# Row maxima of an attention stage transferred in two halves of key heads

## What is computed

```python
x = x + _L0_attn_ref(_layernorm(x), ...)            # mixer
x = x + _L0_xattn_ref(_layernorm(x), ctx_512, ctx_512)
x = x + _L0_ffn_ref(_layernorm(x), ...)             # experts

def _L0_xattn_ref(q, k, v):      # 32 query heads, 8 key heads, 16 wide
    scores = jnp.einsum('bkgsd,bktd->bkgst', qh, kh) * scale
    attn = jax.nn.softmax(scores, axis=-1)
    out = jnp.einsum('bkgst,bktd->bkgsd', attn, vh)
```

## Time and profile before

| | us |
|---|---|
| median of 3 runs | 1469.41 (1467.95 to 1471.85) |
| the profiled execution, whole | 1465.78 |
| its span | 1464.0 |
| attention in it | 699 to 990 |

### The profile page before, as it was taken

One profiled execution on the slowest core, in us unless ns is written; L12 is line 12 of the kernel. 1 busy time (PEld: TensorE's weight loads), 2 busy tenths in 40 slices (PEclk: granted clock), 3 DMA queues, 4 the chain that ended last, 5 costly groups with the idle time before them and its releaser, 6 DMA issues.

```text
span 1464.0 us, 23008 instructions
## 1 busy us (share of the span) xinstructions
PE 1339.8 (92%) x7713; PEld 734.7 (50%) x7713; DVE 877.2 (60%) x1822; ACT 723.4 (49%) x1390; POOL 584.7 (40%) x871
## 2 busy tenths in 40 slices
PE   5799999999999999998788877888999999999997
PEld 4566666666666665654333333323444444444443
DVE  5798898979797979757888888755111111111111
ACT  2666667667666776663676766672111111111110
POOL 1454465555455465774223246143122222222221
PEclk9899999999999999998798988887999999999999
DMA  9000000000000000000210100002343344244322
GB/s 337 9 8 5 7 6 1 12 1 12 1 9 4 8 6 8 17 1 1 97 34 33 35 33 31 30 31 74 115 132 107 79 133 135 51 130 130 58 44 30
DMA packets 40291, 73.00 MB, mean 50 GB/s; under 512 B 18544, under 2 KB 22896, under 8 KB 39152
## 3 DMA queue, kind: packets, MB, share of 16 engines
q1 hardware_dynamic: 30240, 48.10, 9.4%
q0 software_dynamic: 8736, 20.61, 7.3%
q10 hardware_dynamic: 1200, 2.82, 0.5%
HBM read 148.91 MB, written 19.99 MB: 115 GB/s over the span
## 4 chain that ended last, share of the span: by engine, by line
PE 67%; DVE 18%; issue 5%; POOL 3%; ACT 3%; DMA 2%; SPq 1%; POOLq 0%; DVEq 0%; ACTq 0%
PE work_ps L535 13%; PE gate_ps L1524 9%; PE up_ps L1524 9%; PE down_ps L1508 9%; PE work_ps L607 7%; DVE conv L816 6%; PE work_ps L540 3%; PE work_ps L629 3%; DVE maxes L1216 3%; PE work_ps L1042 2%; PE mturn_ps L540 2%; PE decay_ps L1033 2%; PE decay_ps L617 2%; DVE mix L732 2%; DMA qT<-nmaxT 1%
## 5 line engine op out<-in xcount | busy, mean ns | idle before, releaser
L535 PE MATMUL work_ps<-xnT,w_in 128*128 128x256 f32 (+1 forms) x1216 | 301.0, 393 | 2.3 <-DVE xdt L856 1.5
L732 POOL TENSOR_TENSOR mix<-decay,cbm 128x512 f32<-128x512 f32 x128 | 182.1, 1424 | 218.9 <-ACT decay L727 191.0
L535 PEld LDWEIGHTS work_ps<-xnT,w_in 128*128 128x128 f32 (+1 forms) x1216 | 220.2, 189 | 64.9 <-issue 33.7
L723 ACT ACTIVATE decay<-decay_ps 128x512 f32<-128x512 f32 x256 | 154.1, 602 | 111.1 <-PE decay_ps L617 110.5
L1612 POOL DMA_INDIRECT out_dram<-y_out,ids x39 | 61.9, 1587 | 334.3 <-DVE row_w L1576 230.2
L1216 DVE TENSOR_REDUCE maxes<-work_ps 128x2 f32<-128x512 f32 x256 | 166.7, 683 | 42.8 <-PE work_ps L1018 41.8
L816 DVE SCALAR_TENSOR_TENSOR conv<-raw,conv_w,conv 128x256 f32<-128x256 f32 x240 | 179.2, 753 | 7.1 <-ACT conv L683 1.3
L1114 ACT ACTIVATE prob<-decay_ps 128x512 f32<-128x512 f32 x256 | 142.9, 608 | 78.9 <-PE decay_ps L1033 77.5
L1591 DVE TENSOR_TENSOR act<-gelu,up_ps 128x512 f32<-128x512 f32 x39 | 26.8, 688 | 252.1 <-PE up_ps L1524 252.1
L727 ACT ACTIVATE decay<-decay 128x512 f32<-128x512 f32 x256 | 164.0, 641 | 4.7 <-PE work_ps L535 3.0
L1524 PE MATMUL gate_ps<-w_e,xgT 128*128 x312 | 140.5, 593 | 1.4 <-ACT xgT L1541 1.0
(11 more groups left out here) (270 smaller groups left out, 1913.5 us busy)
## 6 DMA issues: line engine op xcount, KB each, us to landing
w_e<-c_experts_dram SPq DMA_DIRECT2D x39, 3072.0 KB
normed_tokens<-r_xn SPq DMA_DIRECT2D x17, 256.0 KB, 2.2
out_dram<-x_sb SPq DMA_DIRECT2D x17, 256.0 KB, 2.5
x_sb<-x_dram SPq DMA_DIRECT2D x1, 3072.0 KB, 16.6
w_in<-c_w_inT_dram ACTq DMA_DIRECT2D x1, 2560.0 KB, 12.3
w_in<-c_w_inT_dram SPq DMA_DIRECT2D x1, 2048.0 KB, 8.8
w_out<-c_w_outT_dram SPq DMA_DIRECT2D x1, 2048.0 KB, 21.6
RT<-cum_scratch SPq DMA_DIRECT2D x32, 48.0 KB
```

The costliest lines, as they stand in the source:

```text
L535: m = e.matmul(ps[0:width, at:at + L], w_in[:, k, col:col + width], xnT[b % 2][:, k, :], start=(k == 0), stop=(k == KD - 1))
L723: e.activation(decay[s % 5][:, :], decay_ps[s % 3][:, :], ACT.Relu, scale=-1.0).then_inc(piece_done[stage], 1)
L732: return e.tensor_tensor(four(mix[s % 5]), four(decay[s % 5]), cb, ALU.mult)
```

## The change

The order of the sweeps becomes key head first, tile second. The maxima of a batch are handed over in two halves h of key heads (0 to 3 and 4 to 7). nmax, n_turn, n_copy and n_out exist once per half: nmax in slots 12 and 28, n_turn in 13 and 29, n_copy and n_out in 14 and 30. Each half has buffers of its own (nmaxT), two transfers of 8 rows each, and a count of its own; the first score of each half of a batch waits for its half.

```diff
--- before.py
+++ after.py
@@ -42,6 +42,7 @@
 ITEMS = [(kh, par, t, quad) for kh in range(2) for par in range(2) for t in range(TPB) for quad in range(4)]
 ODD = [(quad + par) % 2 for kh, par, t, quad in ITEMS]
 LEAD = 5
+HALF = QH // 2
 NORMED = [(0, 2, -44, 0), (2, 4, -43, 1), (4, 8, 4, 2), (8, 16, 37, 5)]
 ROUTED = [(3, 0, 8), (5, 8, 12), (6, 12, 14), (7, 14, 16)]
 ROUND = 1.5 * 2.0 ** 23 * P
@@ -49,7 +50,8 @@
 def sweeps():
-    left = [[(t, k) for t in range(TPB) for k in range(KVH)] for odd in range(2)]
+
+    left = [[(t, k) for k in range(KVH) for t in range(TPB)] for odd in range(2)]
     order = []
     for p in range(len(ITEMS)):
         odd = 1 - ODD[(p - LEAD) % len(ITEMS)]
@@ -246,8 +248,10 @@
             put(r + 17 + 5 * t, ("q_copy_v", b, t, 0), ("q_turn", b, t, 1))
             put(r + 19 + 5 * t, ("q_copy_s", b, t, 1))
             put(n * (b - 1) + 6 + t, ("v_in", b, t))
-        put(n * (b - 1) + n - LEAD + 1, ("nmax", b), ("n_turn", b))
-        put(n * (b - 1) + n - LEAD + 2, ("n_copy", b), ("n_out", b))
+        for h in range(2):
+            put(n * (b - 1) + n // 2 * (h + 1) - LEAD + 1, ("nmax", b, h))
+            put(n * (b - 1) + n // 2 * (h + 1) - LEAD + 2, ("n_turn", b, h))
+            put(n * (b - 1) + n // 2 * (h + 1) - LEAD + 3, ("n_copy", b, h), ("n_out", b, h))
         if b == 1:
             put(2, ("first_expert",))
         for g in range(4):
@@ -456,7 +460,7 @@
             v_aug = [sb(st, f"v_aug{i}", [P, TPB, KVH, 32]) for i in range(2)]
             maxes = [sb(st, f"maxes{i}", [P, TPB, QH]) for i in range(2)]
             nmax = [sb(st, f"nmax{i}", [P, TPB, QH], F16) for i in range(2)]
-            nmaxT = [sb(st, f"nmaxT{i}", [QH, L], F16) for i in range(2)]
+            nmaxT = [[sb(st, f"nmaxT{i}_{h}", [HALF, L], F16) for h in range(2)] for i in range(2)]
             ctx.append(sb(st, "ctx2", [P, TPB, KVH, DH]))
             qT = [sb(st, f"qT{i}", [P, NPR, L], F16) for i in range(2)]
             kT = [sb(st, f"kT{i}", [P, KVH, L], F16) for i in range(2)]
@@ -1018,17 +1022,17 @@
                     m = e.matmul(work(*piece)[:, hh * L:(hh + 1) * L], qT[b % 3][base:base + PARTS, 2 * k + hh, t * P:(t + 1) * P], kT[b % 3][base:base + PARTS, k, :], start=True, stop=True)
                 m.then_inc(piece_done[stage], 1)
             elif stage == "n_turn":
-                b, = key
-                e.wait_ge(*done("nmax", b))
+                b, h = key
+                e.wait_ge(*done("nmax", b, h))
                 for t in range(TPB):
-                    m = e.transpose(work16(*piece)[0:QH, t * P:(t + 1) * P], nmax[b % 2][:, t, :], ident16[:, :])
+                    m = e.transpose(work16(*piece)[0:HALF, t * P:(t + 1) * P], nmax[b % 2][:, t, h * HALF:(h + 1) * HALF], ident16[:, :])
                 m.then_inc(piece_done[stage], 1)
             elif stage == "score":
                 s, = key
                 b, (kh, par, t, quad) = s // N_ITEMS, ITEMS[s % N_ITEMS]
                 base, k = SLOT * ODD[s % N_ITEMS], 4 * kh + quad
-                if s % N_ITEMS == 0:
-                    e.wait_ge(load_max, 32 * (b + 1))
+                if s % (N_ITEMS // 2) == 0:
+                    e.wait_ge(load_max, 32 * (2 * b + kh + 1))
                 e.wait_ge(*(done("exponent", s - 3) if s >= 3 else done("bound", NS_STEPS - 1)))
                 e.matmul(score_ps[s % 3][:, :], kT[b % 3][base:base + PARTS + 1, k, t * P:(t + 1) * P],
                          qT[b % 3][base:base + PARTS + 1, 2 * k:2 * k + 2, :], start=True, stop=True).then_inc(piece_done[stage], 1)
@@ -1211,21 +1215,22 @@
             elif stage == "max_fold":
                 b, p = key
                 t, k, odd = SWEEPS[p]
-                first = NPR * odd + 2 * k
+                first = HALF * (k // 4) + HALF // 2 * odd + 2 * (k % 4)
                 e.wait_ge(*done("max", b, p))
                 e.reduce_max(maxes[b % 2][:, t, first:first + 2], work("max", b, p)[:, :].rearrange("p (h t) -> p h t", h=2), AX.X).then_inc(piece_done[stage], 1)
             elif stage == "nmax":
-                b, = key
-                e.wait_ge(*done("max_fold", b, N_ITEMS - 1))
+                b, h = key
+                cs = slice(h * HALF, (h + 1) * HALF)
+                e.wait_ge(*done("max_fold", b, N_ITEMS // 2 * (h + 1) - 1))
                 if b >= 2:
-                    e.wait_ge(*done("n_turn", b - 2))
-                e.tensor_scalar(nmax[b % 2][:, :, :], maxes[b % 2][:, :, :], -1.0, None, ALU.mult).then_inc(piece_done[stage], 1)
+                    e.wait_ge(*done("n_turn", b - 2, h))
+                e.tensor_scalar(nmax[b % 2][:, :, cs], maxes[b % 2][:, :, cs], -1.0, None, ALU.mult).then_inc(piece_done[stage], 1)
             elif stage == "n_copy":
-                b, = key
-                e.wait_ge(*done("n_turn", b))
+                b, h = key
+                e.wait_ge(*done("n_turn", b, h))
                 if b >= 2:
-                    e.wait_ge(load_max, 32 * (b - 1))
-                e.tensor_copy(nmaxT[b % 2][:, :], work16("n_turn", b)[0:QH, 0:L]).then_inc(piece_done[stage], 1)
+                    e.wait_ge(load_max, 32 * (2 * (b - 2) + h + 1))
+                e.tensor_copy(nmaxT[b % 2][h][:, :], work16("n_turn", b, h)[0:HALF, 0:L]).then_inc(piece_done[stage], 1)
             elif stage == "pv_out":
                 b, g = key
                 kh, par = g // 2, g % 2
@@ -1451,12 +1456,13 @@
                 e.dma_start(tile_id[:, :], A["c_tile_id"]).then_inc(load_m, 16)
                 e.dma_start(w_e[:, 0, :, :], expert_dram[:, 0, :, :]).then_inc(load_e[0], 16)
             elif stage == "n_out":
-                b, = key
-                e.wait_ge(*done("n_copy", b))
+                b, h = key
+                e.wait_ge(*done("n_copy", b, h))
                 for odd in range(2):
                     row = SLOT * odd + PARTS
-                    e.dma_start(qT[b % 3][row:row + 1, :, :], nmaxT[b % 2][odd * NPR:(odd + 1) * NPR, :]).then_inc(load_max, 16)
-                e.wait_ge(load_max, 32 * (b + 1))
+                    e.dma_start(qT[b % 3][row:row + 1, h * NPR // 2:(h + 1) * NPR // 2, :],
+                                nmaxT[b % 2][h][odd * NPR // 2:(odd + 1) * NPR // 2, :]).then_inc(load_max, 16)
+                e.wait_ge(load_max, 32 * (2 * b + h + 1))
             elif stage == "out_in":
                 b, t = key
                 tile = b * TPB + t
```

## The result

The changed kernel took 1461.96 us in the median (1454.37 to 1468.88, 16 runs) against 1467.74 us (1464.36 to 1476.60, 16 runs) of the kernel before on the same chip: ratio 0.9948, 95% interval 0.9928 to 0.9968. Two further series of it gave 0.9909 (0.9873 to 0.9945) and 0.9952 (0.9928 to 0.9976). The ratio is formed from all the runs and is not that of the two medians, which stand 5.8 us apart. So it is faster by 0.5%, 7 to 8 us, where 3.9 us were forecast.

A forecast was written before the change was run, and what follows sets the result against it. No engine's total was the bound; engines go in lockstep by slots, so shared idle time counts. Gains of 5.85 us less losses of 1.9 us gave 3.9 us faster: 1465.5 us against the 1469.4 us median, range 1460.5 to 1472.5 us.

The forecast's parts named there:

- That the wait goes, and is hidden: First scores' 8.2 us PE wait for transferred maxima ends; the earlier transfers hide behind 18 slots of other work, costing nothing.
- What it is worth: At the first scores of batches, the smaller of PE's and DVE's idle time counts: 4.95 us gained, bounds 4.2 to 8.2.
- n_turn a slot later: At a batch's end n_turn stands behind pv_turn, which waits for pv_copy: taken as 0, bounds 0 and 3.4 us.
- batch 5: Score and max can run ahead there until DVE idles at 887.03: 0.9 us gained, bounds 0 and 2.96.
- The added pieces: Extra nmax (0.10 us for a half) and n_copy (0.2 us) per batch: 0.3 us of DVE for each of eight batches.
- mixer: Half 0 of batch 0 falls into the mixer's tail: 0.3 us of DVE and 0.1 for a bank lost.
- Mid-batch: Slots 12 to 16: n_turn waits 1.0 us, product comes 0.7 us later; less the cover by r_xn's wait, 1.2 us lost.
- The clock: TensorE's low-clock stretch, batch 1 against batch 3, costs some 0.2 us; effect under 1.5 us for seven batches.
- Rival A: All of PE's idle comes back, since DVE catches up in later gaps: 7.2 us faster, 1462.2 us; chance 0.28.
- the signs that were named for it: Batches 2 and 4 shorter by 1.6 us or more would speak for Rival A.
- Rival C: n_turn at slot 13 is paid in full in all six batches with r_stats: 7.1 us slower, 1476.5 us; chance 0.11.
- r_xn did not start over 1 us late: Sign in mid-batch: r_xn itself starting over 1 us later would make the prediction wrong the way of Rival C.

## Why the prediction was right or wrong

**That the wait goes, and is hidden: right.** No score waits; the transfer leaves at slot 14 or 30. The first score of batch 1, to be read against the earlier trace rows:

```profile
732.32 0.17 DVE L1227 TENSOR_SCALAR nmax<-maxes 128x32 f16<-128x32 f32 x1
...
733.14 0.63 PE L544 MATMUL work_ps<-ident,pv 128*128 128x128 f32 x4 [0.68 <-DVE maxes L1220]
...
733.70 0.28 PE L1028 MATMUL work_ps<-ident,nmax 128*16 128x128 f16 x2
...
734.02 0.28 DVE L1233 COPY nmaxT<-work_ps 16x256 f16<-16x256 f16 x1 [0.33 <-PE work_ps L1028]
...
735.80 4.27 DVE L1220 TENSOR_REDUCE maxes<-work_ps 128x2 f32<-128x512 f32 x7
```

**What it is worth (4.95 us; bounds 4.2 to 8.2): too high for the wait alone.** It gave 2.4 us at equal clock. The working compared idle times of PE and DVE at the first scores only. As the lines show, DVE's gap of 1.47 us is gone there, but PE now waits 0.68 us for a fold ahead of pv_turn, a wait that was for nmax before; over the attention its waits for folds at L544 went from 1.9 us (1 wait) to 6.0 us (9). The sum treated the batch's end as if nothing but the transfer could be late.

**n_turn a slot later (0), batch 5 (0.9): not contradicted.** With the wait gone, the slot later gave 0.9 +- 0.9 us (1459.8 against 1460.7), which agrees with 0.9 and hardly differs from nothing. With the wait in place it cost 4.8 +- 2.4 us at equal clock (ratio 1.0071).

**The added pieces (0.3 us per batch, mixer 0.4): too high, if anything.** The half nmax took nearly as long as the whole, not 0.10 us, and the copy 0.27 to 0.28 us. The groups of DVE's line of nmax, after (each half: 176 ns in the mean; before, whole: 185 ns):

```profile
L1227 DVE TENSOR_SCALAR nmax<-maxes 128x32 f16<-128x32 f32 x16 | 2.8, 176 | 0.0
```

Yet with all of half 0's pieces and no mid-batch wait the kernel takes 1462.8 +- 0.6 us, without them 1463.0 +- 0.9. The Trainium skill, VectorE: DVE Perf Modes, "The TRN2 errata", gives 58 cycles and the elements divided by the factor of a perf mode (the prediction left the factor out), and says beside the table that the measured fixed part is about 150 cycles. With 150 cycles and a factor of 2, an estimate is 173 ns for a half and 190 for the whole; the traces have 176 and 185 ns, where the prediction's reading gave 94 and 127.

**Mid-batch (1.2 us lost): each mechanism right, the sign wrong.** This is the step that failed. Batch 1, to be read against the earlier trace rows:

```profile
747.66 0.18 DVE L1227 TENSOR_SCALAR nmax<-maxes 128x32 f16<-128x32 f32 x1
...
747.99 0.27 PE L1028 MATMUL work_ps<-ident,nmax 128*16 128x128 f16 x2 [1.22 <-DVE nmax L1227]
...
748.36 0.68 DVE L1210 COPY kT<-work_ps 128x1024 f16<-128x1024 f16 x1
...
749.09 1.83 PE L1046 MATMUL work_ps<-prob,v_aug 128*32 128x512 f32 x8 [0.21 <-DVE kT L1210]
...
753.04 0.66 PE L544 MATMUL work_ps<-ident,r_xn 128*128 128x128 f32 x4
```

n_turn waits 1.22 us (1.0 forecast), the product is released by kT's copy and starts 13.6 us after the batch's first score instead of 12.7 (0.7 later forecast), and the wait for r_xn is gone. What that does to the time was not a loss of 1.2 us but, by the runs at equal clock, a gain of 3.0. The term counted how late PE's product comes and left out where PE's low clock, and DVE's idle time beside it, would then fall.

**The clock (0.2 us): the term mis-sized.** I took it from one pair, batches 1 and 3 of the earlier trace rows, with a stretch of 3.3 us just where DVE is full. There the price is nearly nothing, as the fit says too. The same length four us later makes a batch 1.1 to 1.6 us longer, and 13.4 us of it from 18.4 us on made batch 1 38.7 us long in one of the wait-free kernels (the batch, and that stretch):

```profile
736.20:774.90 38.70, 33.42 (x255) 16.01 (x252) 28.25 (x69) 26.50 (x50) 10.44 (x24) 0.82 0.09 32
754.60:768.00 13.40, 13.40 (x71) 7.32 (x68) 5.17 (x13) 5.53 (x10) 0.00 (x0) 0.50 0.23 76
```

By the Trainium skill, TensorE: Matmul & The Clock Gate, "What's actually happening", removed waits should raise the clock and a new one lower it. The runs show neither in that simple form: taking the wait away alone left the mean at 0.9507 against 0.9527 of before, and the kernels with the mid-batch wait have 0.954 to 0.956. What counted more was where the low stretches lay.

**The sum.** At equal clock 1465.9 - 2.4 (wait) - 0.7 (the step to the kernels whose n_turn of half 0 doesn't wait, within the scatter) - 3.0 (mid-batch wait) = 1459.8 us; 2.0 us more come with the higher mean clock (0.9547 against 0.9527). The forecast of 3.9 us lay near the first two together, 3.1, by two errors that partly cancel, and so by luck: the wait was overrated, and of the 1.9 us at which the pieces and their places were priced none was found. The rest is the mid-batch wait. The terms also don't stand by themselves. Taken the other way round, with the wait put back into the changed kernel, the additions cost 3.3 us and the removal gives 9.4: beside a wait for the transfer nothing is seen of what the mid-batch wait gives. Rival A named a size close to the result (7.2 us) for another reason, all of PE's idle time coming back; batches 1 to 3, the signs that were named for it (batch 2 stayed at 37.9 us, batch 4 lost 0.4) and the 2.4 us speak against it. Rival C, slower by that very wait, was the opposite of what happened, and r_xn did not start over 1 us late (in batch 1 16.5 us after the first score, 0.6 later than before).

**What stays open:** why the low stretches lie earlier in the kernels whose n_turn or score waits for half 0's nmax and not in the one whose score waits for r_stats, what the PSUM banks add, and why the removed wait is worth 9.4 us in one kernel and 2.4 in the other.

## What to carry to other kernels

Price a removed wait by taking it away alone (stale data transferred early are enough), not by PE's idle time at that place: 8.2 us of idle were worth 2.4 here at equal clock. Then put it back into the finished kernel too, as here (9.4 us): the two prices differ when waits work on each other. Where several engines go in lockstep, ask of every wait and every stretch at a low clock which engine is full beside it; in this stage a us of PE at the low clock beside a full DVE cost 0.03 us, and 0.35 us a few slots on. And compare small changes over many runs with their mean clocks beside them: two series of nearly the same kernel stood 0.5% apart in their medians and level at the same clock.

## What the runs showed of the hardware

- The granted clock differs between executions of one program, 0.943 to 0.961 in the mean over 127 runs, and 0.01 of it goes with 9.8 us of 1466. A clock lower by 0.01 over 1466 us is 29.3 us more at half the rate, so that is 0.33 us for each us at the lower level, near the 0.35 and 0.40 us of the fit behind the cheap place.
- The same program runs the same place now at one level, now at the other: batch 6 of the changed kernel held 3, 7 and 17 us at 1.2 GHz in three profiles and took 29.8, 31.2 and 35.4 us. In both profiles of the kernel before it held 13.7 us and took 34.7.
- The product of eight matmuls took 1.06 us at the high level and 1.94 us at the low one; a score 0.39 and 0.60 us.
- nmax over 32 elements of a partition (16 heads of two tokens) takes 176 ns, over 64 (32 heads of two tokens) 185 ns, and the copy of 16 rows takes as long as that of 32 (0.27 us).
